# First attention of a four-layer kernel: copies of the head outputs, products with v, transposes of the maxima and lead of the maxima rearranged

## What is computed

```
q = (x @ Wq).reshape(b, s, H, HD).transpose(0, 2, 1, 3)      # b 2, s 1024, H 16, HD 8
k = jnp.repeat((x @ Wk)..., GROUPS, axis=1)                  # 4 key heads, each for 4 heads
v = jnp.repeat((x @ Wv)..., GROUPS, axis=1)
attn = jnp.einsum('bhqd,bhkd->bhqk', q, k) * scale
attn = attn + slopes[None, :, None, None] * rel[None, None, :, :]
attn = jax.nn.softmax(attn, axis=-1)
out = jnp.einsum('bhqk,bhkd->bhqd', attn, v)
```

## Time and profile before

| what | value |
|---|---|
| three runs | 818.02, 821.1, 821.12 us, median 821.1 us |
| profiled execution | 816.93 us, of which 815.1 us are the span of its instructions |
| mean granted TensorE clock | 0.913 of 2.4 GHz |
| busy | TensorE 686.1 us, VectorE 634.2 us, ScalarE 441.2 us, GpSimd 156.0 us |
| first attention, from the first maxima to the last copy of outputs | 29.2 to 386.6 us |

### The profile page before, as it was taken

One profiled execution on the slowest core, in us unless ns is written; L12 is line 12 of the kernel. 1 busy time (PEld: TensorE's weight loads), 2 busy tenths in 40 slices (PEclk: granted clock), 3 DMA queues, 4 the chain that ended last, 5 costly groups with the idle time before them and its releaser, 6 DMA issues.

```text
span 815.1 us, 16597 instructions
## 1 busy us (share of the span) xinstructions
PE 686.1 (84%) x5846; PEld 438.3 (54%) x5846; DVE 634.2 (78%) x1148; ACT 441.2 (54%) x974; POOL 156.0 (19%) x287
## 2 busy tenths in 40 slices
PE   7489888888888888889983698669999998998883
PEld 4223232323332332234752577569999997997652
DVE  1687999999999999961475465789999996554996
ACT  3137888888888888887461236411121114454442
POOL 7200000000000000000432005811111112122563
PEclk9657999999999999999995559679999999999998
DMA  6801111111111110000726630000000000000000
GB/s 192 222 21 32 31 32 30 32 31 30 32 32 31 32 31 3 2 3 1 207 60 180 149 86 3 0 1 2 1 1 0 0 0 0 1 0 1 14 13 27
DMA packets 19329, 31.87 MB, mean 39 GB/s; under 512 B 4928, under 2 KB 12480, under 8 KB 17920
## 3 DMA queue, kind: packets, MB, share of 16 engines
q1 hardware_dynamic: 17920, 29.42, 13.7%
q0 software_dynamic: 1344, 1.58, 0.7%
HBM read 23.25 MB, written 7.34 MB: 38 GB/s over the span
## 4 chain that ended last, share of the span: by engine, by line
PE 55%; ACT 18%; DVE 11%; issue 7%; DMA 4%; POOL 3%; SPq 2%; DVEq 0%; ACTq 0%; POOLq 0%
ACT probs L1150 15%; PE ps_hi L730 14%; PE ps_lo L980 7%; PE ps_hi L743 7%; PE ps_lo L982 6%; PE ps_lo L981 6%; PE ps_hi L1040 2%; DVE mx L1447 2%; DVE probs L1730 2%; DMA q_rep<-mrow 1%; PE ps_hi L912 1%; PE ps_hi L1031 1%; ACT big L1103 1%; PE ps_lo L877 1%; PE ps_hi L792 1%
## 5 line engine op out<-in xcount | busy, mean ns | idle before, releaser
L1447 DVE TENSOR_REDUCE mx<-ps_lo 128x2 f32<-128x1024 f32 x256 | 308.5, 1224 | 25.2 <-PE ps_lo L705 21.1
L1150 ACT ACTIVATE probs<-ps_hi 128x512 f32<-128x512 f32 x512 | 276.7, 592 | 55.4 <-PE ps_hi L730 39.6
L730 PE MATMUL ps_hi<-q,k 28*128 28x512 f32 x512 | 133.0, 514 | 44.1 <-ACT probs L1150 31.4
L743 PE MATMUL ps_hi<-probs,v_blk 128*32 128x256 f32 x2048 | 166.4, 411 | 0.2 <-ACT probs L1150 0.2
L705 PE MATMUL ps_lo<-k,q 26*128 26x512 f32 x512 | 137.7, 534 | 8.7 <-DVE mx L1447 5.9
L1664 DVE SCALAR_TENSOR_TENSOR tok_cur<-ps_lo,w_cur,tok_cur 128x384 f32<-128x384 f32 x240 | 127.4, 612 | 5.7 <-PE ps_lo L982 4.9
L730 PEld LDWEIGHTS ps_hi<-q,k 28*128 28x128 f32 x512 | 50.0, 189 | 151.3 <-ACT probs L1150 125.8
L980 PE MATMUL ps_lo<-w_hi,op_hi 128*128 128x384 f32 (+1 forms) x304 | 107.6, 354 | 19.9 <-DVEq L1625 10.1
L981 PE MATMUL ps_lo<-w_lo,op_hi 128*128 128x384 f32 (+1 forms) x304 | 105.1, 346 | 0.0
L982 PE MATMUL ps_lo<-w_hi,op_lo 128*128 128x384 f32 (+1 forms) x304 | 105.0, 346 | 0.0
L743 PEld LDWEIGHTS ps_hi<-probs,v_blk 128*32 128x32 f32 x2048 | 45.2, 111 | 64.4 <-ACT probs L1150 50.6
(11 more groups left out here) (224 smaller groups left out, 831.0 us busy)
## 6 DMA issues: line engine op xcount, KB each, us to landing
q<-q_parts SPq DMA_DIRECT2D x32, 192.0 KB
q_rep<-q_parts SPq DMA_DIRECT2D x8, 576.0 KB
k<-k_parts SPq DMA_DIRECT2D x32, 96.0 KB
k_rep<-k_parts SPq DMA_DIRECT2D x24, 96.0 KB
q_parts<-qk_hi SPq DMA_DIRECT2D x8, 256.0 KB, 4.1
q_parts<-qk_p SPq DMA_DIRECT2D x12, 128.0 KB, 3.2
xa<-in_L_attn_x SPq DMA_DIRECT2D x4, 256.0 KB, 3.2
q_parts<-qk_lo SPq DMA_DIRECT2D x4, 256.0 KB, 4.8
```

The source lines that it names most:

```text
L730: mm = pe.matmul(bank(4 + (2 * n + a) % 3), k0[rows, k_at:k_at + P], q0[rows, h * QN:(h + 1) * QN], start=True, stop=True)
L743: mm = pe.matmul(o_bank()[32 * r:32 * r + 32, 0:OW], v_all[:, at:at + 32], probs0[:, n % P_RING, r * OW:(r + 1) * OW], start=(kb == 0), st ...
L1150: act.activation(probs0[:, n % P_RING, a * QN:(a + 1) * QN], bank(4 + (2 * n + a) % 3), ACT.Exp).then_inc(s0_free, 1)
L1447: dve.reduce_max(mx2[:, j % 2, :, i, kh], bank(2 * (m % 2), 2).rearrange("p (a n) -> p a n", a=2), AX_X).then_inc(max0_done, 1)
```

## The change

Five things, all in the first attention. `AHEAD` is 14 in place of 18. The products with v come one unit per step from step 2 on. `max_T` is a plain matmul with the identity, moved from the end of the step with kb 1 to the end of the step with kb 3, where it writes its columns of bank 7 while the head's accumulation is open (its start flag is set for the first head only). ScalarE copies the head outputs between the two exps of the unit with kb 1, and the row of maxima after both exps of the unit with kb 3. VectorE's `head_max` stands directly behind the eighth reduction of its head.

```diff
-AHEAD = 18
+AHEAD = 14
...
             def max_T(j):
                 pe.wait_ge(mx_parts_set, j + 1)
-                if j == 1:
-                    pe.wait_ge(mrow0_set, 1)
-                pe.transpose(o_bank()[0:2 * KB, OW:OW + P], mx_parts[:, j % 2, :].bitcast(F32), ident_sb[:]).then_inc(
-                    mx_T_ps, 1)
+                pe.matmul(o_bank()[0:2 * KB, OW:OW + P], mx_parts[:, j % 2, :].bitcast(F32), ident_sb[:],
+                          start=(j == 0), stop=True, skip_group_check=(j > 0)).then_inc(mx_T_ps, 1)
...
                 if kb == 0:
                     pe.wait_ge(o0_free, j)
-                    pe.wait_ge(mrow0_set, min(j + 2, NH))
+                if kb == 2 and j + 1 < NH:
+                    pe.wait_ge(mrow0_set, j + 2)
...
-                if n % KB == 3 and n > 0:
-                    outputs0(n - 3)
-                if n >= 3 and n % KB != 2:
+                if n >= 2:
                     outputs0(n - 2)
-                if n >= -7 and (n + 7) % KB == 0 and (n + 7) // KB < NH:
-                    max_T((n + 7) // KB)
-                at = n - (NU - 14)
+                if n >= -5 and n % KB == 3 and (n + 5) // KB < NH:
+                    max_T((n + 5) // KB)
+                at = n - (NU - AHEAD + 1)
...
             def heads_out(j):
                 act.wait_ge(p0_free, KB * (j + 1))
-                if j + 2 < NH:
-                    act.wait_ge(mx_T_ps, j + 3)
...
                 for a in range(2):
                     act.activation(probs0[:, n % P_RING, a * QN:(a + 1) * QN], bank(4 + (2 * n + a) % 3),
                                    ACT.Exp).then_inc(s0_free, 1)
-                if n % KB == 1:
-                    j = n // KB - 1
-                    if j >= 0:
-                        heads_out(j)
-                    if j + 2 < NH:
-                        max_row(j + 2)
+                    if a == 0 and n % KB == 1 and n > KB:
+                        heads_out(n // KB - 1)
+                if n % KB == 3 and n // KB + 1 < NH:
+                    max_row(n // KB + 1)
...
-                if m % KB == 0 and j:
-                    head_max(j - 1)
-            head_max(NH - 1)
+                if m % KB == KB - 1:
+                    head_max(j)
```

## The result

| what | before | changed |
|---|---|---|
| median | 819.56 us (4 runs, 817.86 to 821.12) | 802.32 us (4 runs, 800.59 to 805.03) |
| ratio | | 0.9848 [0.9809, 0.9887] |
| profiled execution, span | 816.93, 815.1 us | 805.03, 803.2 us |
| mean granted clock | 0.913 | 0.919 |
| start of the last copy of head outputs | 386.22 us | 371.57 us |

The kernel is faster: by 1.5% going by the ratio and the two profiled executions, by 2.1% (17.2 us) going by the two medians. Medians and ranges here are of all executions of a kernel, ratios of its fast ones alone. The forecast of 937 us was wrong by its main step; the rival with the early clock, 804 us by its sum, is what happened.

What follows compares the result with a forecast made beforehand. It took TensorE at 1.2 GHz to bound the changed attention: 48.6 + 419.3 (241 steps) + 15.6 (30 transposes) = 483.5 against 366.20, so 816.93 + 118 = 935, forecast 937 us; likeliest case 926 to 944, full range 815 to 945.

Steps and rivals of the forecast that it cites:

- rival (B): First attention: the clock comes back early, at 72.4 us as before; 804 to 808 us, chance 0.20.
- The step that failed: First attention: without groups of 16 products the clock stays at 1.2 GHz until about unit 243, +117.3 us.
- The second half of the step: First attention: plain steps of 1.74 us, one unit's products each, never bring the clock back up.
- The falls: First attention: four falls of the clock, following the step without products, go with it; 4 times 1.34 us, 5.4.
- The head at 2.4 GHz: One head at the higher clock: 9.52 + 0.09 + 0.12 + 0.13 = 9.86 us instead of 10.03; bounds 9.6 and 10.1.
- The copy of the outputs inside the unit: ScalarE, between the two exps: waits for the same step's products and makes the next exp late by 0.12 us.
- The transpose: TensorE, moved into a step with products: two records as a plain matmul, costing 0.13 us per head at the higher clock.
- The row of maxima: ScalarE: copied two units later, where slack is 1.19 us minus two exps; costs nothing.
- The step into the next head: Scores at the head boundary, 217.90 to 219.18: takes 0.09 us more than a plain step.
- `head_max`: VectorE: waits for the reduction just ahead, 0.1 to 0.2 us per head, covered by 0.7 us of slack; costs nothing.
- The head at 1.2 GHz: One head at the lower clock: 8 x 1.74 + 0.52 = 14.44 us with two records per transpose.
- The start: Scores of unit 0, fourteen ahead: start at 45.6 us instead of 48.46, a gain of 2.8, with stores queued behind loads.

Runs made afterwards that it cites:

- experiment 1: Changed kernel with the transpose of the maxima in transpose mode again, at its new place: 864.52 and 825.8 us.
- experiment 2: The same kernel as experiment 1, run again on another chip: 801.09, 806.63, 864.57 and 919.27 us.
- experiment 4: Changed kernel with the transposes in transpose mode, plus an unread plain 16-column matmul behind the products of the step with kb 6: 799.04 us, 0.9785.
- experiment 3: The changed kernel itself, run again as a control: 800.66 us, 0.9841.
- experiment 5: Changed kernel with an unread plain 16-column matmul added in steps 2 and 4 to 8: 801.36 us, 0.9823.
- experiment 9: Changed kernel with the head outputs copied after both exps of the unit with kb 1: 804.25 us, 0.9884.
- experiment 10: Changed kernel with `head_max` back behind the first reduction of the next head: 809.0 us, 0.9912.
- experiment 6: Kernel before the change, with the transpose of the maxima as a plain matmul at its old place: 807.93 us, 0.9929.
- experiment 7: Changed kernel with no products with kb 2 and two units' with kb 3, plain transpose behind them: 812.23 us, 0.9972.

## Why the prediction was wrong, and where it was right

**The step that failed** is "no group of 16 products is left ... By the rows, what brought the clock back has been removed". For the kernel before the rows do say that: plain steps at 0.50 with a matmul in flight for 8.00 of 8.00 us, five recoveries behind five double groups. But the same timeline has a sixth group of 16 at the lower clock, earlier in the first head of the kernel before, which I passed over:

```profile
53.95 1.94 PE L743 MATMUL ps_hi<-probs,v_blk 128*32 128x256 f32 x16
55.81 0.79 PE L730 MATMUL ps_hi<-q,k 28*128 28x512 f32 x2
```

It is as long as the one at 68.78, and the clock stayed at 0.50 behind it for another 17 us, through the very stretch of 56 to 64 us. So the group was not enough by itself either, and the claim on what brings the clock back rested on less than it seemed. What I overlooked besides is the other new thing in that place, the plain transpose. I counted it as a second record of 0.21 us and never asked what it does to the clock. Its price at the clock stood at nothing without a reason. Experiments 1, 2 and 4 show that it matters: in transpose mode the six executions took 801 to 919 us; with a plain matmul behind a unit's products somewhere in each head, the 24 executions with a lead of 14 and the new products (changed kernel, experiments 3, 4, 5 and 9) took 796.6 to 809.6. Experiment 10, with a plain transpose and a head 0.22 us longer, took 802.4 to 819.0, which is still below the four longest of the six. The only difference between experiment 1 and the changed kernel is the mode of 32 matmuls.

The second half of the step, that a plain stretch never brings the clock back, fell as well, in experiments 1 and 2: it did, at 267.1 and at 53.4 us, in kernels without a group of 16 and without a plain transpose. The plain transpose makes an early return far more likely here; it is not needed for one. Five recoveries behind a double group are a correlation of a kernel that has such a group in every head; the one plain stretch of a head was no proof of "never". Why the same steps end the low stretch once at 53 and once at 267 us, I could not settle.

**The rule of the Trainium skill.** The granted clock of experiment 1 is 0.50 through 137.00 us of 137.00 busy. The Trainium skill, "TensorE: Matmul & The Clock Gate", section "What's actually happening", has activity release the throttle; by busy records this kernel contradicts it: a matmul in flight all the time was not enough here. The same page of the Trainium skill, section "Part 4: PE-mode transpose", says that a matmul in transpose mode does not count as busy in the same way and that the full clock does not engage for it. Experiments 1, 2 and 4 agree as far as they go: 801 to 919 us with the mode, 796.6 to 801.7 with the mode and one plain matmul per head. They do not show that the mode is the reason, since the two forms differ in length as well, and the clock came up at 53.4 and at 267.1 us with the mode too. I weighed the first rule of that page of the Trainium skill and not this one, which bore on the change.

**The falls** were foreseen to go, 5.4 us, and went. Their reason was only half right. I ascribed them to the step without products. Experiments 6 and 7 keep that step and, with a plain transpose, have no fall in their profiles; experiments 1 and 2, once their clock is up, have uniform products and a transpose in transpose mode, and no fall either. So the plain transpose alone is enough, and so is the rest of the change without it; that the uniform products do it there is argued, since the lead, the copies and `head_max` differ from before as well.

**The head at 2.4 GHz**: 9.86 forecast, 9.89 measured, but by errors that cancel.
- The copy of the outputs inside the unit: 0.12 forecast, 1.37 - 1.19 = 0.18 measured.
- The transpose: 0.13 forecast, 1.20 - 1.19 = 0.01 measured, although it has two records as foreseen. The next scores wait for the exp anyway.
- The row of maxima: "nothing" forecast, 1.27 - 1.19 = 0.08 measured. The products of the next step now wait for its copy ([0.20 <-ACT mrow L1100] in the row at 204.97), by the wait that the change adds for units with kb 2, and the step is 1.27.
- The step into the next head: 0.09 forecast, 1.28 - 1.19 = 0.09 measured.
- `head_max`: "nothing" forecast, against its old place. VectorE's own wait is covered, but with 14 tiles of lead the new place saves 0.22 per head (experiment 10). That it would save less with a lead of 18 is argued from the wait for GpSimd, not tried. What I missed is the chain behind it: reduction, GpSimd's split, transpose.

**The head at 1.2 GHz**: 14.44 forecast for two records; the step with the transpose is 2.15 us (experiment 5), 0.41 above 1.74 instead of 0.52, so 14.33. (By the rows as shown 59.30 - 57.55 is 1.75; four plain steps, 57.55 to 64.52, give 1.74.) With one record it is 14.23 as the rows gave.

**The start**: 45.6 forecast, 44.66 measured, a gain of 3.8 instead of 2.8 (48.46 - 45.6 is 2.9). The stores did not wait for the load of the earlier trace rows: issued at 41.21 they were through in time for scores at 44.66, before the 45.4 at which that load was said to land; in the changed kernel it was issued at 37.41 and landed 7.7 us later, at 45.1.

**The rival (B)** gave 804 us and the point from which the clock decides, three heads. Its sum came near in part by luck: start 2.4 (3.8 measured in the profile), heads 5.1 (3.9), falls 5.4, and none of the 2.8 given back behind the attention. The point comes out again with the numbers of experiment 2: 813.6 - 801.1 = 12.5 us are 2.9 heads of 4.34. What was wrong was its chance, 0.20. I supported it by the length of the attention and by a rule of the Trainium skill, while its mechanism stood in the diff.

## What to carry to other kernels

Where a forecast hangs on the clock, go through every matmul that the change adds, moves or gives another mode and ask of each what it does to the clock, even if its own time is a fifth of a microsecond. That all recoveries stand behind one pattern shows what may bring the clock up, not what alone can; run the kernel with the suspected instruction in its other mode before believing either. A kernel whose clock is decided by chance shows it only over many executions: the two fastest of six here would have told that the mode is harmless.

## What the runs showed of the hardware that was not expected

- A float32 transpose of 128x16 as a plain matmul (two records, 0.38 us together at the higher clock) and in transpose mode (one record, 0.28 us) cost the same time in a step at the higher clock (1.20 and 1.21 us; at the lower 2.15 and 2.05), but not the same clock: with the plain one none of 20 executions (changed kernel, experiments 3, 5 and 9) took more than 809.61 us, with the mode alone four of six were above 825.
- TensorE with a matmul in flight all the time can stay at 1.2 GHz for 201 us on end (66 to 267 in experiment 1) and then come up without any change in what it does.
- Of two equal groups of 16 products early in the kernel before, 1.94 us each at the lower clock, the second was followed by the higher clock (68.78, up at 72.7 us), the first was not (53.95).
- The plain transpose did not bring the clock up each time or at once. The first in a head's step started at 51.11 us in experiment 3 and at 50.73 in experiment 9, and the clock was up at 53.8 and 52.9; in the changed kernel and with a lead of 18 it was the second, with the clock up at 65.9 and 70.7. What decides between them these runs don't show.
